# A vision tower's residual kept without its mean, and another order in its expert loop

## The reference

```python
h = tok(x)                                  # patches @ W + b, class token, positions
# attention block, low-rank factors
y  = layernorm(h) * g1 + b1
h1 = h + softmax(causal(Q(y) @ K(y).T / 4)) @ V(y) @ out_U @ out_V + out_b
y2 = layernorm(h1) * g2 + b2
h2 = h1 + gelu_tanh(y2 @ fc1_U @ fc1_V + fc1_b) @ fc2_U @ fc2_V + fc2_b
h3 = layernorm(h + h2)                      # no gain, no bias
# mixture: 15 experts, 3 per token, and a shared expert; gelu-gated
out = layernorm(h3 + sum_k comb[k] * expert_k(h3) + shared(h3))
```

## Time and profile before

| | |
|---|---|
| median of 3 runs | 240.78 us (240.02 to 243.75) |
| profiled execution | 240.42 us, of which span 238.6 us |
| mean granted TensorE clock | 0.993 |
| PE busy | 220.6 us, 92% |
| ACT busy | 95.5 us, 40% |
| DVE busy | 98.5 us, 41% |
| POOL busy | 107.1 us, 45% |
| products of the `L344` helper on the chain that ended last | 76% |

### The profile page before, as it was taken

How to read it: one execution, slowest core, us unless ns; L and a number is a source line. 1 busy time by engine, 2 the same in 40 slices (tenths; PEclk the granted TensorE clock), 3 DMA queues, 4 the chain that set the end, 5 groups by cost and what they waited for, 6 DMA issues and landing times.

```text
span 238.6 us, 4515 instructions
## 1 busy us (share of the span) xinstructions
PE 220.6 (92%) x1605; PEld 142.4 (60%) x1605; DVE 98.5 (41%) x261; ACT 95.5 (40%) x215; POOL 107.1 (45%) x149
## 2 busy tenths in 40 slices
PE   7999899888997899999999989999999999999991
PEld 4776577677776577777877734444444444444670
DVE  3155432679962521243678845222222212121043
ACT  2003546476782694345231523243433424333132
POOL 0130028388420699999900360644546464333100
PEclk9999999999997999999999999999999999999999
DMA  7999999000004980000110040398435222201552
GB/s 234 400 347 390 347 413 414 28 4 3 3 0 150 420 355 0 3 0 3 44 58 0 26 110 3 99 325 320 168 119 198 66 69 66 66 25 44 180 193 81
DMA packets 11648, 34.43 MB, mean 144 GB/s; under 512 B 2426, under 2 KB 4139, under 8 KB 11628
## 3 DMA queue, kind: packets, MB, share of 16 engines
q1 hardware_dynamic: 9612, 28.65, 32.0%
q0 software_dynamic: 2016, 5.51, 7.6%
HBM read 25.43 MB, written 4.01 MB: 123 GB/s over the span
## 4 chain that ended last, share of the span: by engine, by line
PE 84%; ACT 8%; issue 3%; DVE 2%; DMA 2%; ACTq 0%
PE ps L344 76%; ACT cT L746 3%; PE ps L1646 3%; PE ps L1445 2%; DMA embed_sb<-embed 2%; ACT pair_mem L679 1%; ACT pair_mem L673 1%; PE ps L1455 1%; DVE ln_mem L848 1%; ACT xn L605 0%; PE ps L1563 0%; PE ps L1399 0%; PE ps L1327 0%; DVE ln_mem L835 0%; ACT ln_mem L588 0%
## 5 line engine op out<-in xcount | busy, mean ns | idle before, releaser
L344 PE MATMUL ps<-wres,cT 128*64 (+1 forms) x360 | 63.8, 465 | 0.4 <-DVE cT L1239 0.4
L344 PEld LDWEIGHTS ps<-wres,cT 128*64 128x64 f32 (+1 forms) x360 | 26.2, 131 | 29.2 <-issue 24.2
L568 POOL DMA_INDIRECT y_dram<-ln_mem,dest_i x21 | 20.8, 989 | 40.0 <-ACT ln_mem L759 39.7
L559 POOL DMA_INDIRECT embed_sb<-x_dram,gather_i x21 | 20.7, 986 | 20.5 <-DVE gather_i L1164 14.4
L1232 DVE TENSOR_TENSOR h<-ps,h 128x256 f32<-128x256 f32 x21 | 8.9, 425 | 47.1 <-issue 31.0
L529 POOL TENSOR_SCALAR wres<-wres,mult 128x256 f32<-128x256 f32 x30 | 27.1, 915 | 0.0
L753 ACT ACTIVATE h<-ps 128x256 f32<-128x256 f32 x21 | 8.1, 385 | 42.4 <-PE ps L344 38.3
L357 POOL TENSOR_TENSOR wres<-wres,cst_sb 128x148 f32<-128x148 f32 x24 | 10.9, 481 | 23.2 <-DVE wres L868 20.8
L344 PE MATMUL ps<-h,stage 128*128 128x296 f32 x64 | 17.7, 417 | 0.0
L344 PE MATMUL ps<-bias_t,fac_mem 96*64 96x512 bf16 x42 | 8.5, 403 | 5.8 <-ACT cT L746 5.3
L490 POOL TENSOR_TENSOR wres<-wres,cst_sb 128x111 f32<-128x111 f32 x32 | 11.1, 378 | 6.1 <-PE ps L1455 6.1
(11 more groups left out here) (194 smaller groups left out, 393.0 us busy)
## 6 DMA issues: line engine op xcount, KB each, us to landing
wres<-experts SPq DMA_DIRECT2D x15, 768.0 KB, 13.6
embed_sb<-embed SPq DMA_DIRECT2D x6, 416.0 KB, 5.4
wres<-ut SPq DMA_DIRECT2D x3, 768.0 KB, 9.2
stage<-shared SPq DMA_DIRECT2D x2, 771.0 KB, 13.6
wres<-y_dram SPq DMA_DIRECT2D x4, 384.0 KB, 4.5
stage<-wres SPq DMA_DIRECT2D x2, 512.0 KB
f1v<-fc_v SPq DMA_DIRECT2D x1, 512.0 KB
f2u<-fc_u SPq DMA_DIRECT2D x1, 512.0 KB
```

The costliest lines, as they stand in the source:

```text
L344: return nc.tensor.matmul(o, w, x, start=start, stop=stop)
L559: pool.indirect_dma_start(out=xg[:, i % NXG], out_offset=None, in_=x_dram[:, :], in_offset=bass.IndirectOffsetOnAxis(ap=gather_i[:, column ...
L568: pool.indirect_dma_start(out=y_dram[:, :], out_offset=bass.IndirectOffsetOnAxis(ap=dest_i[:, column(i):column(i) + 1], axis=0), in_=ys[:, ...
```

## The change

1. The residual loses its mean once. Only the first norm keeps `mean` and `centre`; `xc` is then used in place of `h0` for the residual (L917, L524). The weights that feed the residual (`ov_sb`, `f2v`) are centred over their features by two sums and two multiply-adds on DVE (`centre_weights`, after the composing), and the two biases (`out_b`, `fc2_b`) by a small product on PE (`bias_means`) and a subtraction on DVE (`centre_biases`).
2. The second and third norm have no `mean` and no `centre`. Squares are taken from `h1` and `hs` themselves, chunk by chunk, and `var` waits for each chunk by itself.
3. `spread` splits its four products: two read partitions 0 to 63 and write one bank, two read partitions 64 to 127 and write the next. `scale` reads both banks.
4. ACT's steps of the second norm stand elsewhere: the root of the first half goes before the last context copy; squares and root of the second half go before the gelu table is loaded, so two `warm(Sqrt)` and the filler between blocks 3 and 4 go.
5. In the expert loop `second(i - 2)` goes behind both transposes on PE, and `tile_in(i + 1)` before `tile_out(i - 2)` on ACT. At the end `second(NT - 2)` goes before `gated_transposed(NT - 1)`.

```diff
-        ln1, ln2, ln3 = Norm("ln1", 6, 7), Norm("ln2", 2, 3), Norm("ln3", 0, 1)
+        ln1, ln2, ln3 = Norm("ln1", 4, 6), Norm("ln2", 2, 2), Norm("ln3", 0, 0)
...
-                pool.tensor_tensor(half(hs, n), half(h0, n), half(h1, n), ALU.add).then_inc(sum_done, 1)
+                pool.tensor_tensor(half(hs, n), xc[:, n], half(h1, n), ALU.add).then_inc(sum_done, 1)
...
-            def squares(ln, n):
-                act.wait_ge(ln.cen, n + 1)
-                nc.scalar.activation(sq[:, n], xc[:, n], ACT.Square).then_inc(ln.sq, 1)
+            def squares(ln, n, src, made, each):
+                for c in range(DC):
+                    act.wait_ge(made, DC * n + c + 1 if each else n + 1)
+                    nc.scalar.activation(sq[:, n, c], src[:, c], ACT.Square).then_inc(ln.sq, 1)
...
             over_pairs(act.Fori, turn)
-            squares(ln2, 0)
+            squares(ln2, 0, half(h1, 0), op_done, True)
+            std(ln2, 0)
             context_out(PAIRS - 1)
-            std(ln2, 0)
             affine_act(ln2, 0, C_LN2G, C_LN2B)
+            squares(ln2, 1, half(h1, 1), op_done, True)
+            std(ln2, 1)
             warm(ACT.Gelu_apprx_tanh)
...
                 mlp_gelu(g)
-                if g == 0:
-                    squares(ln2, 1)
-                if g == 1:
-                    warm(ACT.Sqrt)
-                    std(ln2, 1)
-                if g == 3:
-                    affine_act(ln2, 1, C_LN2G, C_LN2B)
+                if g in (2, 3):
+                    affine_act(ln2, 1, C_LN2G, C_LN2B, (g - 2,))
                 if g == 12:
-                    squares(ln3, 0)
-            warm(ACT.Sqrt)
+                    squares(ln3, 0, half(hs, 0), mo_done, True)
             std(ln3, 0)
...
                 gate(i)
+                if i + 1 < NT:
+                    tile_in(i + 1)
                 if i >= 2:
                     tile_out(i - 2)
-                if i + 1 < NT:
-                    tile_in(i + 1)
...
+            def centre_biases():
+                dve.wait_ge(res_mm, 1)
+                nc.vector.tensor_tensor(
+                    res_b[:, :, :], vec[:, C_RES:C_RES + 2 * DC].rearrange("p (c v) -> p c v", c=DC),
+                    ps[:, 3, 0:2].unsqueeze(1).to_broadcast([P, DC, 2]), ALU.subtract).then_inc(res_done, 1)
+
+            def centre_weights():
+                dve.wait_ge(ld_out, 32)
+                nc.vector.tensor_reduce(w_sum[0:RO, 0:2], ov_sb[:, :, :], AX.X, ALU.add).then_inc(w_cen, 1)
+                dve.wait_ge(ld_mlp, 96)
+                nc.vector.tensor_reduce(w_sum[:, 2:3], f2v[:, :], AX.X, ALU.add).then_inc(w_cen, 1)
+                dve.wait_ge(w_cen, 1)
+                nc.vector.scalar_tensor_tensor(
+                    ov_sb[:, :, :], w_sum[0:RO, 0:2].unsqueeze(2).to_broadcast([RO, 2, D]), -1.0 / D, ov_sb[:, :, :],
+                    ALU.mult, ALU.add).then_inc(w_cen, 1)
+                dve.wait_ge(w_cen, 2)
+                nc.vector.scalar_tensor_tensor(
+                    f2v[:, :], w_sum[:, 2:3].to_broadcast([P, D]), -1.0 / D, f2v[:, :],
+                    ALU.mult, ALU.add).then_inc(w_cen, 1)
...
-            centre(ln1, 0, h0)
-            centre(ln1, 1, h0)
+            centre(0)
+            centre(1)
+            centre_biases()
...
             composed_out(2)
+            centre_weights()
...
-                if ahead == 0:
-                    centre(ln2, 0, h1)
...
+            def bias_means():
+                for c in range(DC):
+                    last = mm(ps[:, 3, 0:2], ones_d, vec[:, C_RES + 2 * c:C_RES + 2 * c + 2], c == 0, c == DC - 1)
+                last.then_inc(res_mm, 1)
...
             def spread(ln, n):
 
                 pe.wait_ge(ln.rs, n + 1)
-                for q in range(NQ):
-                    last = mm(ps[:, ln.banks[n], q * QT:(q + 1) * QT], spr[:, q * P:(q + 1) * P],
-                              rs[:, n])
+                for q in (0, 2, 1, 3):
+                    rows, bank = slice(QB * (q // 2), QB * (q // 2 + 1)), ln.banks[n] + q // 2
+                    last = mm(ps[:, bank, q % 2 * QT:(q % 2 + 1) * QT], spr[rows, q * P:(q + 1) * P], rs[rows, n])
                 last.then_inc(ln.bc, 1)
...
+            pe.wait_ge(res_done, 1)
+            pe.wait_ge(ld_out, 32)
+            pe.wait_ge(w_cen, 3)
             for c in range(DC):
                 for k in range(2):
                     last = mm(ps[:, 3, c * D:(c + 1) * D], ou_sb[:, k, c * P:(c + 1) * P],
...
-                if ahead == 0:
-                    mean(ln2, 0, h1, op_done, 2)
...
             first_low(0)
-            mean(ln2, 1, h1, op_done, 4)
+            var(ln2, 1)
             hidden(0)
             hidden(1)
+            spread(ln2, 1)
             for g in range(2, NH * FIC):
                 hidden(g)
                 second_low(g - 2)
-                if g == 2:
-                    var(ln2, 1)
-                if g == 3:
-                    keep_clock(1, 8)
-                    spread(ln2, 1)
...
-                if g == 11:
-                    mean(ln3, 0, hs, mo_done, 2)
...
             spread(ln3, 0)
-            mean(ln3, 1, hs, mo_done, 4)
-            keep_clock(3, 4)
+            keep_clock(7, 4)
...
                 first(i)
-                if i >= 2:
-                    second(i - 2)
                 if i + 1 < NT:
                     tile_transposed(i + 1)
                     lower_expert(i + 1)
                 if i >= 1:
                     gated_transposed(i - 1)
+                if i >= 2:
+                    second(i - 2)
+            second(NT - 2)
             gated_transposed(NT - 1)
-            second(NT - 2)
             second(NT - 1)
```

More of the change, by code:

```diff
@@ L600, in _, with affine_act @@
             warms = iter(range(WARMS))
-            def affine_act(ln, n, gamma, beta):
-                for c in range(DC):
+            def affine_act(ln, n, gamma, beta, chunks=(0, 1)):
+                for c in chunks:
                     act.wait_ge(ln.out, DC * n + c + 1)
@@ L611, in _ @@
             warm(ACT.Sqrt)
-            squares(ln1, 0)
-            squares(ln1, 1)
+            squares(ln1, 0, xc[:, 0], centred_h0, False)
+            squares(ln1, 1, xc[:, 1], centred_h0, False)
             std(ln1, 0)
@@ L831, in _, with centre, spread_out, by_bank @@
                         ALU.add, ALU.add).then_inc(emb_done, 1)
-            def centre(ln, n, src):
-                dve.wait_ge(ln.mean, n + 1)
+            def centre(n):
+                dve.wait_ge(mean_mm, n + 1)
                 nc.vector.tensor_tensor(
-                    xc[:, n], half(src, n),
-                    ps[:, ln.banks[n], 0:HT].unsqueeze(1).to_broadcast([P, DC, HT]),
-                    ALU.subtract).then_inc(ln.cen, 1)
+                    xc[:, n], half(h0, n),
+                    ps[:, 6 + n, 0:HT].unsqueeze(1).to_broadcast([P, DC, HT]),
+                    ALU.subtract).then_inc(centred_h0, 1)
+            def centre_biases():
[16 more added lines that the diff above has]
+                    ALU.mult, ALU.add).then_inc(w_cen, 1)
+            def spread_out(ln, n):
+                return ps[:, ln.banks[n]:ln.banks[n] + 2, 0:2 * QT]
+            def by_bank(x):
+                return x.rearrange("p (b t) -> p b t", b=2)
             def inverse_std(ln, n):
@@ L943, in _ @@
             inverse_std(ln2, 0)
-            scale(ln2, 0)
+            scale(ln2, 0, half(h1, 0))
             attention_out(1)
@@ L962, in _ @@
             z1_out(0)
-            centre(ln2, 1, h1)
             inverse_std(ln2, 1)
-            scale(ln2, 1)
+            scale(ln2, 1, half(h1, 1))
             z1_out(1)
@@ L1285, in keep_clock, with mean @@
                     mm(ps[:, bank, 0:HT], fill[:, 0:P], fill[:, :])
-            def mean(ln, n, src, made, count):
+            def mean(n):
                 for c in range(DC):
-                    pe.wait_ge(made, count - DC + c + 1)
-                    last = mm(ps[:, ln.banks[n], 0:HT], ones_d, src[:, c, n * HT:(n + 1) * HT], c == 0, c == DC - 1)
-                last.then_inc(ln.mean, 1)
+                    pe.wait_ge(emb_done, 2 * n + 3 + c)
+                    last = mm(ps[:, 6 + n, 0:HT], ones_d, h0[:, c, n * HT:(n + 1) * HT], c == 0, c == DC - 1)
+                last.then_inc(mean_mm, 1)
+            def bias_means():
+                for c in range(DC):
+                    last = mm(ps[:, 3, 0:2], ones_d, vec[:, C_RES + 2 * c:C_RES + 2 * c + 2], c == 0, c == DC - 1)
+                last.then_inc(res_mm, 1)
             def var(ln, n):
-                pe.wait_ge(ln.sq, n + 1)
                 for c in range(DC):
+                    pe.wait_ge(ln.sq, DC * n + c + 1)
                     for q in range(NQ):
@@ L1342, in _ @@
             pe.wait_ge(ld_cst, 16)
-            mean(ln1, 0, h0, emb_done, 4)
-            mean(ln1, 1, h0, emb_done, 6)
+            mean(0)
+            mean(1)
+            bias_means()
             compose(0)
```

40 lines of the change are left out of this document (21 added, 19 removed).

## The result

The changed kernel took 229.01 us (median of 4, 228.47 to 231.08), the kernel before 242.26 beside it (4 runs, 240.02 to 243.9): a ratio of 0.9536, 95% interval 0.9457 to 0.9615. The forecast was 228.3, range 225.0 to 232.9. The profiled execution took 229.41 us, its span 227.6 against 238.6, at a mean granted clock of 0.981 against 0.993. In the changed kernel the helper `mm` is L350, the copies of the loop L749 and L762, the transposes L1673 and L1717, the chunkwise squares L595.

What follows compares the result with a forecast made beforehand. PE was taken as the bound, with 84% of the chain of waits. Terms 6.0 + 0.45 + 3.4 + 1.0 + 1.1 + 0.5 = 12.45 off 240.42 gave 228.0, with the median's 0.36 228.3 us; range 225 to 232.9.

Steps and rivals of the forecast that it cites:

- Loop: Expert loop: ACT's copy of the transposed tile is hidden, 18 rounds at 0.33, -6.0 us, range 4.8 to 6.5.
- The sequencer: Expert loop: PE's register read between transposes falls behind by x per round, giving 234.3 + 18x; chance 0.03.
- the late gathers: Expert loop: gathers queued behind later scatters could cost PE their lateness; a lead of over 6 us was to cover it.
- the kept round: Expert loop: another wait (drain, late gather) takes the place, 234.3 us, chance 0.05; half way there, 231.3, chance 0.07.
- Tail: Loop's end: PE ends some 0.5 later, but POOL's scatter queue swallows it: 0, range 0 to +0.3.
- Spreads: Norms: products on two 64-row halves overlap, -0.45 per spread, bounds 0 and 0.5; rival of no gain, 230.5, chance 0.14.
- First norm: First norm: bias product +0.45, two halved spreads -0.45 each, DVE's weight centring just hidden; net -0.45, bounds +0.45 and -0.9.
- Last turn and second norm: Last pair turn and second norm's first half: context leaves 0.8 sooner, spread at 1.2 GHz halved for 0.8; -1.6.
- MLP to block 4: MLP up to hidden block 4: norm steps, filler and two table loads gone, another -1.8; -3.4 with the last turn.
- rival 1: MLP: clock falls once more to 1.2 GHz for 3.3 us, losing 1.7 to 3.3: 230 to 231.6; chance 0.17.
- a low clock appears in the MLP: Sign named in advance that would show the forecast wrong, beside loop rounds staying above 3.7 us.
- Third norm: Third norm: first half's mean gone -1.0, `unit(0)` earlier at the MLP's end -1.1, second spread shorter -0.5.

Runs made afterwards that it cites:

- the second group's profile: The unchanged changed kernel run again beside three variants of it: 227.66 us, ratio 0.9534 to the kernel before.
- the executions with filler: Changed kernel with unused products in the tail, three before the last second layer and three behind each residual sum; bias product also moved in one: 228.53 and 228.63 us.
- old-tail kernel: Changed kernel with the old order of the expert loop's last three steps, gated_transposed(20) before second(19) again: 229.48 us, ratio 0.9512.

## Why the prediction was right, step by step

The time and the sign were right, and the mechanism of every large term was the one forecast. That 228.3 stood so near 229.01 is partly luck. At full clock the steps give 10.7 where the sum had 12.45: it had 0.7 too much in the loop, 0.6 in the second norm, 0.3 in the third and 0.1 in the first. In the profiled execution the longer low clock took another 1.05, and the early start, which no step of mine had, gave 1.1 back. The medians beside each other differ by 13.3, more than the steps account for; the kernel before had 242.26 there, not the 240.78 that the forecast stood on. The bounds that I named for the terms reach from 226.6 to 232.1; the 225 has no working behind it.

1. **Loop, forecast -6.0, measured -5.3.** The wait went, as said, 0.33 a round. Of the 0.36 read from the starts I had left 0.03 for "the change back from full transposes to half-width tiles"; the half-width products took 0.06 more on top of the 0.33, of which the rest of the round gave 0.02 back. So the term was sized 0.04 a round too high. The sequencer, the late gathers and the kept round (rivals 3 and 4) did not appear.
2. **Tail, forecast 0 (0 to +0.3), measured +0.1 to the end.** The scatter did get later, 5.16 us after the last gelu instead of 4.85, and it is released by ACT (0.86), no longer only by POOL's issue as in the earlier trace rows. The queue swallowed less than I said; the old order has it at 4.70.
3. **Spreads, forecast -0.45 each, measured -0.14 to -0.44 by starts (-0.34 by the rows' lengths).** I took the scores' rate, near the bound of full overlap. Behind a wait it holds; between full-width products most of it is lost.
4. **First norm, forecast -0.45, measured -0.33.** The bias product cost 0.33 on the path instead of 0.45. The first spread gave back 0.15 of that; the second came 0.08 sooner and gave 0.44. DVE's centring was 1.93 instead of 2.6: two sums and two multiply-adds in 0.67, 0.41, 0.68 and 0.41, 1.3 ns a column (1.93 for 1536), not the 1.7 of the residual's operation. That operation reads PE's bank and these don't; whether this is the reason was not tried.
5. **Last turn and second norm, forecast -1.6.** At full clock -1.02, in the profile -0.92 (8.10 to 7.18 from the value product to `first_low`). The output projection, which waits for the context copy, came 0.80 sooner, exactly as said. The other 0.8 was the spread at the low clock; at full clock it gives 0.14.
6. **MLP to block 4, forecast -3.4 in all, measured -2.83 at full clock and -1.8 in the profile.** Behind `first_low` the forecast 1.8 is what full clock shows (7.95 to 6.14, 1.81); the rest is point 5. The missing 1.05 is rival 1: the low clock lasted 6.8 us, not 3.3. It had 0.17. I had also named "a low clock appears in the MLP" as a sign of being wrong, and in the profiled execution it did, over `first_low` until 78.9. It is not a property of the new order: the second group's profile of the same kernel shows full clock there. The Trainium skill (TensorE: Matmul & The Clock Gate, What's actually happening) makes the clock a matter of activity. No run here shows that for the second norm; in the tail the executions with filler lean that way, but the clock also fell there while PE had no wait.
7. **Third norm, forecast -1.0, -1.1, -0.5, measured -1.07, -0.97, -0.24.** The last is mostly point 3 again.

## What to carry to other kernels

Read a stall from start to start, and after a reordering measure the whole round: here the products behind the transposes took back an eighth of the gain. Read a shortened group in the same way, from the group before it to the group behind it: halved spreads gained 0.44 behind a wait and 0.15 between full-width products. A mean product of 1.0 us taken off the bound engine gave 0.1 until ACT's steps were moved ahead of its table load, and 1.8 with both: a removed step only uncovers the next wait of a relay. Where executions of one kernel differ in mean clock, compare profiles stretch by stretch, and look for a stretch at the start that the change cannot have touched.

## What the hardware did that I had not expected

- The granted clock of one and the same program fell in some executions and not in others, in the second norm, in the tail, or in neither; in one group the changed kernel took 229.06 and 229.40 us at a mean clock of 0.982, and 227.53 at 0.997.
- It fell in the tail while PE was issuing products without a gap: in the old-tail kernel the float32 sums went from 0.71 for four records to 1.22, at a granted clock of 0.50, and PE shows no wait from 190 to 212 us.
- With eighteen products that nobody uses, spread through 10 us of the tail, none of 12 executions had a mean clock under 0.990; with eight, spread in the same way, two of six were at 0.981. Whether the products did it stays open, and if so, whether it is their number or their density.
- A group of eight records on two row halves started 0.59 us behind a full-width group, the same group on full rows 0.49.
